# Moving the small steps of units 12 to 15 from GpSimd to VectorE and ScalarE, with a new instruction sequence

## What is computed

```
for each chunk of 128 tokens of a sequence:
    g  = grad of |silu(k W1) W2 - v|^2 at the chunk's first state   # per token
    g  = g * min(1 / |g|, 1)                                        # clipped by its norm
    S_t = eta_t S_(t-1) - theta_t g_t ;  W_t = (1 - alpha_t) W_(t-1) + S_t
    out_t = silu(q_t W1_t) W2_t
out = out @ Wo ; out = out * rsqrt(mean(out^2) + 1e-6) * norm_g * gate
x   = layernorm(x + out)
expert = argmax(x @ gate_w)                                         # one of 8 per token
x   = layernorm(x + x @ expert_w[expert])
```

## Time and profile before

| | us |
|---|---|
| median of 3 runs | 538.97 |
| lowest, highest | 535.79, 542.7 |
| the profiled execution | 540.94 |
| its span, first to last instruction | 539.7 |

### The profile page before, as it was taken

How to read it: one execution, slowest core, us unless ns; L and a number is a source line. 1 busy time by engine, 2 the same in 40 slices (tenths; PEclk the granted TensorE clock), 3 DMA queues, 4 the chain that set the end, 5 groups by cost and what they waited for, 6 DMA issues and landing times.

```text
span 539.7 us, 11103 instructions
## 1 busy us (share of the span) xinstructions
PE 449.3 (83%) x3506; PEld 342.1 (63%) x3506; DVE 385.9 (72%) x1146; ACT 305.8 (57%) x780; POOL 337.7 (63%) x451
## 2 busy tenths in 40 slices
PE   6885999999999989999987979976988776727752
PEld 4564687676687767868756747665766655526641
DVE  4667788898899898988877886987754654523432
ACT  2553367666758658577563846764763663415453
POOL 2004655659778868886785675863576766464547
PEclk9986999999999999999997989996997997987887
DMA  7353162454663555846444636386546654356411
GB/s 231 105 165 116 45 156 91 104 143 93 151 192 71 167 107 144 195 81 170 114 123 103 166 104 143 85 254 166 159 128 169 151 167 139 123 171 181 142 51 60
DMA packets 61353, 73.20 MB, mean 136 GB/s; under 512 B 17293, under 2 KB 48206, under 8 KB 61296
## 3 DMA queue, kind: packets, MB, share of 16 engines
q1 hardware_dynamic: 51616, 46.78, 31.7%
q0 software_dynamic: 8848, 25.44, 18.2%
q10 hardware_dynamic: 832, 0.27, 0.2%
HBM read 44.19 MB, written 19.22 MB: 118 GB/s over the span
## 4 chain that ended last, share of the span: by engine, by line
PE 50%; DVE 13%; POOL 11%; issue 9%; another core or an unknown queue 5%; ACT 5%; SPq 4%; DMA 3%; POOLq 0%; ACTq 0%; DVEq 0%
PE bank L517 8%; PE bank L618 7%; PE bank L538 4%; PE bank L1324 4%; DVE kq_in L567 3%; POOL sorted_rows L1099 3%; POOL out L1369 2%; PE bank L970 2%; PE bank L1031 2%; DVE y L990 2%; PE both L929 2%; PE both L1324 1%; PE both L931 1%; PE bank L809 1%
## 5 line engine op out<-in xcount | busy, mean ns | idle before, releaser
L1369 POOL DMA_INDIRECT out<-os,xs_token x71 | 71.0, 1000 | 40.7 <-issue 14.9
L1099 POOL DMA_INDIRECT sorted_rows<-rows,index x64 | 74.9, 1171 | 23.7 <-issue 15.6
L567 DVE SCALAR_TENSOR_TENSOR kq_in<-shared,conv_w,kq_in 128x256 f32<-128x256 f32 x144 | 69.5, 538 | 10.5 <-ACT kq_in L558 10.4
L517 PE MATMUL bank<-front 128*64 128x256 f32 x512 | 61.8, 394 | 5.3 <-DMA front<-in_w_kv 4.8
L1324 PE MATMUL bank<-shared,front 128*128 x212 | 56.1, 413 | 11.3 <-issue 5.0
L618 PE MATMUL bank<-front 128*128 128x256 f32 x256 | 63.0, 391 | 0.8 <-ACT gate L586 0.8
L1324 PEld LDWEIGHTS bank<-shared,front 128*128 128x128 f32 x212 | 41.9, 207 | 19.6 <-issue 14.0
L618 PEld LDWEIGHTS bank<-front 128*128 128x128 f32 x256 | 47.7, 196 | 8.9 <-issue 3.2
L517 PEld LDWEIGHTS bank<-front 128*64 128x64 f32 x512 | 37.2, 141 | 24.5 <-DMA front<-in_hidden_t 5.5
L1329 DVE BATCH_NORM_STATS2 st<-bank 128x6 f32<-128x256 f32 x53 | 20.2, 422 | 40.7 <-remote 24.6
L1023 ACT ACTIVATE rows<-y,rstd 128x256 f32<-128x256 f32 x64 | 34.3, 592 | 11.2 <-POOL rstd L1017 9.2
(11 more groups left out here) (214 smaller groups left out, 1233.0 us busy)
## 6 DMA issues: line engine op xcount, KB each, us to landing
front<-sorted_rows SPq DMA_DIRECT2D x71, 130.0 KB
front<-in_hidden_t SPq DMA_DIRECT2D x16, 512.0 KB
decay<-gate_clear SPq DMA_DIRECT2D x16, 512.0 KB
y<-in_hidden POOLq DMA_DIRECT2D x16, 512.0 KB
q<-kq_in SPq DMA_DIRECT2D x64, 64.0 KB, 2.9
carry<-carry_rows SPq DMA_DIRECT2D x32, 128.0 KB
hq<-hq SPq DMA_DIRECT2D x64, 64.0 KB
shared<-in_w_expert SPq DMA_DIRECT2D x2, 1024.0 KB, 8.9
```

The lines of the kernel that those rows point to most:

```text
L517: ins = pe.matmul(halves[half(side), kind, :, :], w[:, k, kind * D:(kind + 1) * D], pairs[:, k, side, :, :], start=k == 0, stop=k == KH - 1)
L567: dve.scalar_tensor_tensor(dst, raw[g][:, kind, :, tap:tap + P], conv_w[:, kind, tap:tap + 1], dst, ALU.mult, ALU.add))
L1099: pool.indirect_dma_start(sorted_rows[:, :], bass.IndirectOffsetOnAxis(index[i2][:, b:b + 1], 0), R[:, b, :], None, bounds_check=NE * REGI ...
L1369: pool.indirect_dma_start(out[:, :], bass.IndirectOffsetOnAxis(xs_token[t % LOADS][:, i:i + 1], 0), os_[o][:, i, :], None, bounds_check=TO ...
```

## The change

`late_unit(c, g)` is true for units 12 to 15 (`SMALL_ON_DVE = 12`). For these units:

- In `learn`, norm_p, norm_s, norm_g and weight run on VectorE. The inverse root inv_g stays on GpSimd, as a step of its own.
- In `epilogue`, ms becomes a square root on ScalarE (bias `eps_rms`, a new constant), and rms a reciprocal on VectorE. var becomes a square root on ScalarE; rstd is a reciprocal and shift one fused operation on VectorE; less is gone.
- routed and index run on VectorE.

Waits are added where an engine change needs them. `ORDER` is wholly new: 2388 steps instead of 2376 (three more for each late unit), and the steps of every other unit too stand in other places. The diff of the code, with `ORDER` left out:

```diff
+SMALL_ON_DVE = 12
...
+        eps_rms = sb("eps_rms", [P, 1])
...
+    def late_unit(c, g):
+
+        return n_of(c, g) >= SMALL_ON_DVE
...
-        wait("pool", n("norm_h"))
-        mark("pool", n("norm_p"), pool.tensor_tensor(small[:, 0:2, :], norms[:, 0:2, :], norms[:, 2:4, :], ALU.mult))
-        wait("pool", n("norm_p"))
-        mark("pool", n("norm_s"), pool.tensor_tensor(small[:, 2, :], small[:, 0, :], small[:, 1, :], ALU.add))
-        wait("pool", n("norm_s"))
-        mark("pool", n("norm_g"), pool.tensor_scalar(small[:, 3, :], small[:, 2, :], 1.0, None, ALU.max))
+        who, small_e = ("dve", dve) if late_unit(c, g) else ("pool", pool)
+        wait(who, n("norm_h"), o("weight"))
+        mark(who, n("norm_p"), small_e.tensor_tensor(small[:, 0:2, :], norms[:, 0:2, :], norms[:, 2:4, :], ALU.mult))
+        wait(who, n("norm_p"))
+        mark(who, n("norm_s"), small_e.tensor_tensor(small[:, 2, :], small[:, 0, :], small[:, 1, :], ALU.add))
+        wait(who, n("norm_s"))
+        mark(who, n("norm_g"), small_e.tensor_scalar(small[:, 3, :], small[:, 2, :], 1.0, None, ALU.max))
+        if late_unit(c, g):
+            yield
...
+        if late_unit(c, g):
+            wait("act", *[n(f"ssq{b}") for b in range(NB)], o(f"gated{NB - 1}"))
+            mark("act", n("ms"), act.activation(rms[:, 0, :], ssq[:, :], ACT.Sqrt, bias=v["eps_rms"][:, 0:1], scale=1.0))
+            yield
+            wait("dve", n("ms"), o(f"gated{NB - 1}"))
+            mark("dve", n("rms"), dve.reciprocal(rms[:, 1, :], rms[:, 0, :]))
...
+        if late_unit(c, g):
+            wait("act", n("mv3"), o("shift"))
+            mark("act", n("var"), act.activation(rstd[:, 0, :], mv[:, :, 1], ACT.Sqrt, bias=v["eps_ln"][:, 0:1], scale=1.0))
+            yield
+            wait("dve", n("var"), o("norm"))
+            mark("dve", n("rstd"), dve.reciprocal(rstd[:, 1, :], rstd[:, 0, :]))
+            wait("dve", n("rstd"))
+            mark("dve", n("shift"), dve.scalar_tensor_tensor(rstd[:, 2, :], mv[:, :, 0], -1.0, rstd[:, 1, :], ALU.mult, ALU.mult))
...
-        wait("pool", n("onehot"), n("pos_ps"))
-        mark("pool", n("routed"), pool.tensor_tensor(routed[:, :, :], routed[:, :, :], onehot[:, :, :], ALU.add))
+        who, small_e = ("dve", dve) if late_unit(c, g) else ("pool", pool)
+        wait(who, n("onehot"), n("pos_ps"), o("routed"))
+        mark(who, n("routed"), small_e.tensor_tensor(routed[:, :, :], routed[:, :, :], onehot[:, :, :], ALU.add))
...
+        wait(who, n("where_f"), n("norm"))
+        mark(who, n("index"), small_e.tensor_copy(index[i2][:, :], where_f[:, :]))
```

More of the change, by code:

```diff
@@ L261, in build @@
         pool = nc.gpsimd
-        fills = [(eps_ln[:, :], EPS_LN)] + [(raw[g][:, :, :, 0:3], 0.0) for g in range(G)]
+        fills = [(eps_ln[:, :], EPS_LN), (eps_rms[:, :], EPS_RMS)] + [(raw[g][:, :, :, 0:3], 0.0) for g in range(G)]
         n_raw_fill = len(fills)
@@ L847, in learn @@
             yield
-        wait("pool", n("inv_g"), f"theta0.{n_of(c, g) // 2}", o("grad_w"))
-        mark("pool", n("weight"), pool.tensor_tensor(small[:, 5, :], small[:, 4, :], theta[:, i2, :], ALU.mult))
+        who, small_e = ("dve", dve) if late_unit(c, g) else ("pool", pool)
+        wait(who, n("inv_g"), f"theta0.{n_of(c, g) // 2}", o("grad_w"))
+        mark(who, n("weight"), small_e.tensor_tensor(small[:, 5, :], small[:, 4, :], theta[:, i2, :], ALU.mult))
         yield
@@ L981, in epilogue @@
         yield
-        wait("pool", *[n(f"ssq{b}") for b in range(NB)])
-        wait("pool", o(f"gated{NB - 1}"))
-        mark("pool", n("ms"), pool.tensor_scalar(rms[:, 0, :], ssq[:, :], EPS_RMS, None, ALU.add))
-        wait("pool", n("ms"))
-        mark("pool", n("rms"), pool.tensor_tensor(rms[:, 1, :], rms[:, 0, :], minus_half[:, 0:NB], ALU.pow))
+        if late_unit(c, g):
[4 more added lines that the diff above has]
+            mark("dve", n("rms"), dve.reciprocal(rms[:, 1, :], rms[:, 0, :]))
+        else:
+            wait("pool", *[n(f"ssq{b}") for b in range(NB)])
+            wait("pool", o(f"gated{NB - 1}"))
+            mark("pool", n("ms"), pool.tensor_scalar(rms[:, 0, :], ssq[:, :], EPS_RMS, None, ALU.add))
+            wait("pool", n("ms"))
+            mark("pool", n("rms"), pool.tensor_tensor(rms[:, 1, :], rms[:, 0, :], minus_half[:, 0:NB], ALU.pow))
         yield
@@ L1093, in epilogue @@
         yield
-        wait("pool", n("where_f"), n("norm"))
-        mark("pool", n("index"), pool.tensor_copy(index[i2][:, :], where_f[:, :]))
+        who, small_e = ("dve", dve) if late_unit(c, g) else ("pool", pool)
+        wait(who, n("where_f"), n("norm"))
+        mark(who, n("index"), small_e.tensor_copy(index[i2][:, :], where_f[:, :]))
         yield
@@ L1429 @@
[L1429 to L1432 removed]
+    "p0p0p0p0p0p0p1p0p0p0p0p0p1p0p1p0p0p0p0p0p2p0p0p0p0p1p1p1p1p1p1g0p1p1p0p1p1p1p1p1p1p1s0p1p1p1p1p0p1p0p0p0p0l0p0s0s1l0p1l0"
@@ L1433 @@
+    "x3x4x2x2x4x4x2x1x1x4x3x3x4x4x2x3x3x4x2x4x2x2x1x1x2x4x4x2x1x3x0x2x4x3x4x4x2x1x4x2x2x3x4x0x4x1x3x2x4x2x0x3x1x4x4x2x1x2x3x2"
+    "x1x1x2x2x4x4x1x2x4x3x4x3x0x3x1x2x4x4x3x2x1x2x0x2x1x2x2x4x4x3x3x4x2x2x3x2x4x3x1x4x2x4x4x2x0x2x2x1x2x3x4x4x3x4x4x4x2x0x1x3"
+    "x3x2x4x2x1x1x2x2x0x4x4x1x2x3x2x3x2x4x4x4x2x1x2x3x3x2x4x4x2x2x4x1x3x2x2x4x3x4x4x2x2x3x3x2x4x4x4x4"
 )
```

92 lines of the change are left out of this document (45 added, 47 removed).

## The result

The changed kernel takes 544.77 us (median of 22 runs, 538.81 to 551.61); the kernel before, measured 22 times beside it on the same chip, takes 536.33 us (532.48 to 543.87). The ratio is 1.0129, 95% interval 1.0103 to 1.0155: slower by 1.3% (6.9 us), where 1.2% faster was forecast. The time lies inside the range of 520 to 545, at its edge, and within 2% of no change. The profiled execution of before that the prediction was worked from (540.94 us) turns out to be 4.6 us above the median of these 22; the profiled one of after has a span of 543.5 us and is near its own median.

A forecast was written before the change was run, and what follows sets the result against it. TensorE sets the pace from 50 to 355 us; from 384 to 469 no engine is full, GpSimd's queue crowded at 81%. 540.94 - 1.4 - 5.0 + 1.0 + 0 - 1.0 = 534.5 us, median near 532.5, range 520 to 545.

The forecast's parts named there:

- place 1: First load of the second layer: inv_g replaces the variance root between unit 11's scatters, 1.4 us earlier, bounds 0 and 2.6.
- The tail: From the padding to the end: output t20 before copy t25 moves two issues into GpSimd's gap, 1.0 us less, bounds 0 and 6.6.
- the 5 us of the stage: 384 to 469 us, place 2 included: GpSimd's relief shortens it by 5 us, bounds 0 and 9.2.
- nothing comes through: Rival: ScalarE's in-order outputs and TensorE's products set the stage, additions cancel small gains; 0 change, 538 to 540 us, chance 0.22.
- GpSimd isn't the bound of the tail: Behind unit 15's last scatter: 37 issues take 47.4 us, against 26.2 us of idle time, so GpSimd doesn't limit the tail.
- The new sequence elsewhere: 50 to 355 us: the new order is the same pattern with neighbours swapped, 0 us, bounds -3 and +3.
- the forecast's sign for this: Forecast wrong if TensorE's busy share from 50 to 355 us falls below 93%: then the sequence, not the steps, decides.
- Place 2: Unit 15's chain, last sum of squares to scaling: 3.3 us becomes about 1.0, 2.3 off; profile to show under 1.5.
- Additions: VectorE steps 6.1 us, ScalarE roots 2.4, three more table loads 3.8, mostly covered: 1.0 us on the path, bounds 0 and 12.3.
- The two unknown stretches: Tail stretches of 7.12 and 8.17 us put down to an unknown queue; no part of the change was known to touch them.
- The queue was the limit after all: Rival: GpSimd's queue limits 384 to 469 us; 18.4 us come off, 520.6 us, chance 0.18.
- ScalarE and VectorE take over: Rival: from 355 to 400 us their added work lies on the path, up to +12.3 us, 551.3, chance 0.14.

The follow-up runs named there:

- before_again: The kernel before, unchanged, run once more for a second profiled execution; 512.87 us.
- The spacer: The changed kernel with one unread 128x1 GpSimd operation behind each of the 135 indirect DMA issues; 520.40 us, ratio 1.0148 to before's 512.28 us.
- oldseq_neweng: Small steps of units 12 to 15 moved as in the changed kernel, but in the sequence of before; 512.06 us, ratio 0.9975 to before.
- newseq_oldeng: The changed kernel's new sequence, but the small steps of units 12 to 15 back on GpSimd; 531.64 us, ratio 1.0330 to before.
- old_to_load_new_after: Moved steps, sequence of before up to the first load of sorted rows, new sequence behind it; 504.59 us, ratio 0.9847 to before's 512.87 us.
- after_last: The changed kernel, unedited, on a chip without late updates; 504.16 us, ratio 0.9863 to before's 512.28 us.
- old_to_load_new_after_oldeng: Sequence of before up to the first load of sorted rows, new behind it, small steps back on GpSimd; 541.82 us, ratio 1.0070 to before.
- after_again: The changed kernel, unedited, repeated on another chip; 549.03 us, ratio 1.0212 to before's 539.29 us.
- after_beside: The changed kernel, unedited, as base beside two repairs; 544.51 us, ratio 1.0072 to before's 537.90 us.
- old_to_load_again: The kernel old_to_load_new_after, no line changed, on another chip; 543.81 us, ratio 1.0135 to before's 537.90 us.
- the hybrid: Moved steps, old sequence up to the first load of sorted rows, new behind; ratio 0.9847 as old_to_load_new_after, 1.0135 as old_to_load_again.
- after_rows3: The changed kernel with a third buffer of rows and of indices; 541.75 us, ratio 1.0039 to before's 537.90 us.

## Why the prediction was right or wrong

**The sum, term by term, on A.** The forecast's terms are set here against the two traces of A, stage by stage. The first load was to come 1.4 us earlier (place 1, with 0 for the sequence); it comes 2.0 us later. From there to the padding 5.0 us were to go and up to 1.0 to be added; the stage is 1.3 us longer (100.1 to 101.4). The tail was to lose 1.0 us and is 0.5 longer. So the largest miss is the 5 us of the stage: GpSimd had 10.4 us less to do there, and none of it reached the end. The forecast's own sign for this came up: "wrong if the padding starts no earlier than 468 (nothing comes through)"; it starts at 473.23. So "nothing comes through" tells the stage rightly, but it has no cause for a loss. The loss ahead of the stage is the sequence's, as shown further down.

**On E the size of the gain was right, by luck.** There the changed kernel gains 8.1 us between the medians, the forecast's 6.5 and a little more. But the terms don't match: against before on B the first load comes 5.5 us later and not 1.4 earlier, the stage to the padding is 14.7 us shorter and not 5, outside the bound of 9.2, and the tail is 1.3 us longer. The forecast's reason was half wrong too: I had it that "GpSimd isn't the bound of the tail". On A it is not the earlier trace rows. On E it is, groups of GpSimd from 417 us to the end:

```profile
L1397 POOL DMA_INDIRECT out<-os,xs_token x54 | 52.6, 973 | 16.5 <-issue 7.9 <-ACT os L1392 2.4 <-ACT rs L1375 1.2
L1127 POOL DMA_INDIRECT sorted_rows<-rows,index x10 | 9.8, 980 | 3.1 <-issue 1.2 <-ACT os L1392 0.9 <-DVE st L1357 0.6
```

Those 64 issues follow one another from 417.87 to 499.48 us at a pitch of 1.280 us without a gap; in before_again the last 43 do. The spacer measures it: with it the pitch is 1.403 us, and the last 64 issues run from 429.16 to 518.57. 63 x 0.123 = 7.7 us come from the pitch, 11.3 from the later start, together, but for rounding, the 19.1 us by which the profiled end moves; the medians move by 16.2.

**The second layer is where the chips part.** Windows of before on B, then of the changed kernel on E:

```profile
385.00:470.00 85.00, 66.34 (x458) 52.85 (x456) 51.28 (x279) 50.66 (x126) 65.59 (x80) 0.96 0.61 180
470.00:540.00 70.00, 21.50 (x107) 17.75 (x106) 14.24 (x72) 19.33 (x45) 28.95 (x30) 0.88 0.22 72
```
```profile
385.00:470.00 85.00, 75.72 (x524) 62.16 (x523) 60.32 (x330) 61.03 (x152) 63.78 (x66) 0.98 0.73 215
470.00:540.00 70.00, 13.82 (x67) 10.88 (x65) 10.65 (x54) 13.50 (x32) 22.78 (x24) 0.92 0.12 41
```

TensorE does 524 products there in place of 458 (75.72 us against 66.34), and no more GpSimd time is needed for it (63.78 against 65.59). On A the same change brings 437 products in place of 429, with TensorE busy 66.03 us in place of 63.56. From GpSimd's first output issue to its last the second layer takes 126.6 us on B before and 115.7 on E after (-10.9), but 152.7 and 154.6 on A (+1.9). All times in the next table are from one trace each, from the starts of SyncE's first load and of its padding writes to the end of the span:

| kernel | chip | first load, us | from it to the padding | padding to end |
|---|---|---|---|---|
| before_again | B | 364.0 | 89.6 | 55.3 |
| oldseq_neweng | B | 372.4 | 86.4 | 53.7 |
| newseq_oldeng | B | 380.7 | 94.3 | 55.7 |
| old_to_load_new_after | B | 368.2 | 75.4 | 57.5 |
| after_last | E | 369.5 | 74.9 | 56.6 |
| before | A | 369.8 | 100.1 | 69.7 |
| after | A | 371.8 | 101.4 | 70.3 |
| old_to_load_new_after_oldeng | C | 371.3 | 99.9 | 69.6 |
| after_again | C | 384.7 | 94.7 | 68.3 |
| after_beside | D | 374.6 | 97.5 | 70.1 |
| old_to_load_again | D | 373.3 | 98.5 | 70.9 |

Two of its rows, as the traces of before_again and after_last have them:

```profile
364.03 5.15 SPq L1289 DMA_DIRECT2D front<-sorted_rows  x6
...
453.61 4.42 SPq L1162 DMA_DIRECT2D sorted_rows<-pad_row  x8
```
```profile
369.49 5.01 SPq L1317 DMA_DIRECT2D front<-sorted_rows  x6
...
444.35 4.34 SPq L1190 DMA_DIRECT2D sorted_rows<-pad_row  x8
```

On B and E the stage to the padding falls to 75 us only where the moved steps and the new order behind the first load come together. With the moved steps in the old order it is 86.4 us, and with the new order and the steps on GpSimd 94.3. On A, C and D the same pairing gives 94.7 to 101.4 us, against 99.9 and 100.1 with the steps on GpSimd.

**The new sequence elsewhere, 0: the step that failed, and with it the 5 us of the stage, which were summed as if the order didn't matter.** I priced the sequence by the places I could read and took the rest as neighbours swapped, bounds 3 us. On B it costs 3.3%, 17 us, with the steps on GpSimd (newseq_oldeng), and with them moved, on E, the whole gains 8.1. Nor did the steps by themselves bring the forecast's gain: in the old order they give 0.25%. So steps and sequence can't be priced apart: the steps are worth 0.25% in the old order and, by an estimate across B and E, 4.5% in the new (1.0330 to 0.9863). Part of the price behind the first load can be seen: the new order puts the token counts where VectorE has them ready; GpSimd hasn't. Waits of TensorE, newseq_oldeng, 385 to 480 us:

```profile
PE bank L1175 <- POOL routed L1117: 9.9, 2, 5.0
```

On A the forecast's sign for this, a busy share of TensorE from 50 to 355 below 93%, was nearly reached: it is 284.67 of 305, 93.3%, from 95.1%. On E TensorE is also 3.8 us less busy there than before on B (287.50 against 291.31), and the first output comes 2.9 us later. Where this was lost can be read from TensorE's busy time in two windows, ahead of 280 us and behind it:

| first layer's order | late steps | traces | 50 to 280, us | 280 to 355, us |
|---|---|---|---|---|
| old | GpSimd | before (A), before_again (B), old_to_load_new_after_oldeng (C) | 223.4 to 223.9 | 66.5 to 67.9 |
| old | moved | oldseq_neweng and old_to_load_new_after (B), old_to_load_again (D) | 223.4 to 224.9 | 62.8 to 63.4 |
| new | GpSimd | newseq_oldeng (B) | 218.2 | 68.3 |
| new | moved | after (A), after_again (C), after_beside (D), after_last (E) | 215.1 to 218.9 | 67.7 to 71.6 |

The new order leaves TensorE 4.5 to 9 us of work behind by 280 us, on every chip that ran it: on A 216.3 in place of 223.7 us, 7.3 less, where the forecast had 0 and bounds of 3. It is made up in part later. The moved steps cost 3 to 5 us more behind 280 us in the old order, though the forecast gave all additions 1.0 us on the path. So the first layer loses on both kinds of chip, and only on B and E, where updates come promptly, does the second layer give back more than that.

**Where the gain went on A.** Taking steps off GpSimd moves its issues together: those in unbroken runs of four or more go from 49 of 91 to 70, and the held time behind 355 us from 58.5 to 67.8 us, 9.3 more, enough to cancel a gain like that on E (8.1) but not to turn it into a loss of 6.9. The table of late updates bears it out in one way: the two kernels with the steps on GpSimd have 53.7 and 58.5 us of held time, the eight with moved steps 62.4 to 70.2. But GpSimd's runs grow on B too (58 of 89 to 87 of 91 in the hybrid) and do no harm there, and among the eight the held time doesn't order the ratios (after_rows3 66.5 and 1.0039, old_to_load_again 66.3 and 1.0135). So it is a fit from one profile each and not a proof: why the second layer gives nothing back on A stays open, and so does why the hybrid isn't better than the changed kernel on D, where its TensorE isn't behind at 280 us. A second candidate is the clock. In the stage from 384 to 469 the granted clock, a mean over stretches at 2.4 and at 1.2 GHz, is 0.86 in place of 0.92, and from 485 on 0.73 in place of 0.81; one product takes 151 ns in place of 148 in the first and 243 in place of 234 in the second, 2.5 us of TensorE's time in all by an estimate from these rows. Whether it is cause or consequence of TensorE standing still, no run here parts.

**Place 1, -1.4: not borne out.** The first load comes 2.0 us later, which is less than it varies by itself. inv_g stands in place of the root as predicted, but between unit 11's second and third scatter (362.58 and 364.84), and the last of the scatters that the loads wait for is issued 2.9 us later than before (366.18 against 363.33), with the whole first layer.

**Place 2 and the stage, -5: the steps right, the stage wrong.** From the last sum of squares to the scaling it is 2.5 us (423.08 to 425.55) in place of 3.3, not the under 1.5 that I gave: the root itself is done 0.37 us after the sum (423.45), but the scaling writes the buffer that ScalarE still reads for unit 14's rows, and starts 0.03 us after these are over (425.52). That wait I had not seen. GpSimd's busy time, forecast near 48 us, is 46.60, but the padding, forecast at 462 to 465, comes at 473.23: the relief was there and the stage didn't shorten.

**Additions, +1.0: prices right, exposure too low.** 23 table loads of 1.283 us, as counted; the eight roots take 0.293 us (0.294), the VectorE steps 0.146 to 0.182 (0.17). TensorE waits for none of them among its longest waits, yet in the old order it falls 3 to 5 us behind with them (table above).

**The tail, -1.0.** 70.3 us from the padding to the end, forecast 69 to 70; GpSimd's gap of 6.61 us is 3.35. The two unknown stretches of the earlier trace rows I left out as beyond the change. Their share of the last chain is 5% before and 7% after on A, and there are none in the chains of before_again and after_last. They are of the same kind as the 9.24 us above; how much of the loss they hold isn't shown.

**The rivals.** "The queue was the limit after all" fits B and E: the stage moved by over 8 us, as it asked, but place 1 went the other way, so it came to less than half its price (8.1 of 18.4 us). "ScalarE and VectorE take over" gives the measured sign on A, and with half of its additions even the measured time (545), but not by its mechanism: from 384 to 469 both are at 57% of the stage, and from 355 to 370, its place, VectorE is busy 12.81 of 15 us, less than before (13.70).

## What to carry over

Before taking work off a queue that mostly issues DMAs, read what its issues do to each other: closer issues are a gain only if nobody else stands still while they run, and a wait marked "unknown" or "remote" beside a row of issues can be a price of the change and not noise. A sequence and the placement it was made for are one change; measure both halves alone before pricing either, and on the kind of chip that decides. A time that comes out as forecast proves no term of the sum: check the stages. Take a second trace of one kernel before a shift of a few us is explained. And a result of 1% should be repeated on another chip before it is believed: here its sign turned.

## What the runs showed of the hardware that I had not expected

- The kernel before takes 536.33, 539.29 and 537.90 us on three chips and 512.87, 512.73 and 512.28 us in three sets on two others, 4.6 to 5.3% apart; the granted clock and TensorE's work in the first layer are nearly the same in the traces of A and B (busy 290.15 and 291.31 of 305 us, clock 0.98 and 0.99). Most of the difference lies behind the first load: 170 us on A, 145 on B. The granted clock is lower there too, 0.92 against 0.96 from 385 to 470 us.
- On the first kind, 46 to 66 of TensorE's 460 semaphore updates come 1 to 12.8 us late, nearly all while GpSimd issues indirect DMAs; on the second 0 to 3, at the same pitch of issues.
- SyncE's eight padding writes take 11.81 us to issue beside such a run on A, and 4.42 us on B.
- One 128x1 operation between two indirect issues costs 0.123 us of pitch (1.280 to 1.403) and not its own 0.275 (0.21 to 0.23 in the last run of issues): the 0.30 us between two issues shrinks to 0.17.
